# Value products of two neighbouring pairs issued together in the local attention units

## The reference

```python
# layer 1, x is 8 x 512 x 128
scores = einsum('bhtd,bhsd->bhts', q, k) * 8 ** -0.5
allowed = (j <= i) & (j >= i - 128)
attn = softmax(where(allowed, scores, -inf))
x = layernorm(x + einsum('bhts,bhsd->bhtd', attn, v) @ w_out)
# layer 2
h = layer_norm(x); x1 = x + causal_attention(h) @ w_o
xf = layer_norm(x1); top two of softmax(xf @ w_gate)
x = layernorm(x + x1 + sum over experts of gate * (gelu(xf @ w1 + b1) @ w2 + b2))
```

## Time and profile before

| | us |
|---|---|
| median of three runs | 866.76 |
| lowest and highest | 863.17, 868.02 |
| span of the profiled execution | 868.6 |
| TensorE matmul busy | 655.7 (75%) |
| VectorE busy | 509.7 (59%) |
| ScalarE busy | 462.6 (53%) |
| GpSimd busy | 429.8 (49%) |
| mean granted TensorE clock | 0.897 |

### The profile page before, as it was taken

How to read it: one execution, slowest core, us unless ns; L and a number is a source line. 1 busy time by engine, 2 the same in 40 slices (tenths; PEclk the granted TensorE clock), 3 DMA queues, 4 the chain that set the end, 5 groups by cost and what they waited for, 6 DMA issues and landing times.

```text
span 868.6 us, 19900 instructions
## 1 busy us (share of the span) xinstructions
PE 655.7 (75%) x7512; PEld 393.1 (45%) x7512; DVE 509.7 (59%) x1116; ACT 462.6 (53%) x671; POOL 429.8 (49%) x649
## 2 busy tenths in 40 slices
PE   2557978978887878888788888886614999999900
PEld 0323434434443433444343444442313998898900
DVE  1644667676776888798888879882340222222236
ACT  2035655655674565766677666666502554554503
POOL 4015556556654543245464647458640454445445
PEclk8568999998997998999999999999855999999965
DMA  5635544643643637334362707101014566566464
GB/s 170 157 90 115 138 109 100 154 126 67 159 116 46 153 97 135 102 76 135 66 159 42 185 25 190 43 16 53 20 58 161 187 204 214 184 223 213 168 163 128
DMA packets 73583, 107.45 MB, mean 124 GB/s; under 512 B 8104, under 2 KB 60048, under 8 KB 70428
## 3 DMA queue, kind: packets, MB, share of 16 engines
q1 hardware_dynamic: 68892, 97.86, 42.2%
q0 software_dynamic: 4608, 8.47, 3.3%
HBM read 44.14 MB, written 38.90 MB: 96 GB/s over the span
## 4 chain that ended last, share of the span: by engine, by line
PE 32%; DMA 22%; DVE 17%; issue 10%; SPq 7%; POOL 6%; ACT 4%; another core or an unknown queue 0%; POOLq 0%; ACTq 0%; DVEq 0%
DMA parts_dram<-parts 9%; DMA arena<-parts_dram 7%; PE pair_ps L1415 6%; PE o_ps L1278 6%; SPq L439 4%; PE o_ps L1434 3%; PE pair_ps L1299 3%; PE pair_ps L1198 3%; POOL rows_dram L628 3%; DMA rows_dram<-rows,row_at 3%; PE misc L1434 3%; DVE row_max L878 2%; ACT probs L707 2%; DVE row_max L876 2%; PE pair_ps L1258 1%
## 5 line engine op out<-in xcount | busy, mean ns | idle before, releaser
L707 ACT ACTIVATE probs<-pair_ps 128x1024 f32<-128x1024 f32 x272 | 275.4, 1022 | 116.2 <-PE pair_ps L1198 107.5
L1278 PE MATMUL o_ps<-probs,v_aug 128*32 128x256 f32 (+3 forms) x2048 | 166.0, 421 | 9.1 <-POOL probs L616 3.5
L603 POOL TENSOR_SCALAR_AFFINE_SELECT probs<-probs 128x512 f32<-128x512 f32 x96 | 61.2, 637 | 140.4 <-ACT probs L707 139.4
L1198 PE MATMUL pair_ps<-arena 50*128 50x256 bf16 (+3 forms) x1024 | 108.2, 288 | 26.6 <-DMA arena<-shift_t 6.5
L673 POOL DMA_INDIRECT outputs_dram<-o_norm,arena x80 | 77.7, 971 | 100.5 <-DVE o_norm L1128 80.0
L867 DVE TENSOR_REDUCE row_max<-pair_ps 128x4 f32<-128x768 f32 x96 | 89.7, 953 | 46.7 <-PE pair_ps L1232 46.1
L838 ACT ACTIVATE probs<-pair_ps,arena 128x256 f32<-128x256 f32 x160 | 65.4, 471 | 76.3 <-PE pair_ps L1415 66.0
L876 DVE TENSOR_REDUCE row_max<-pair_ps 128x2 f32<-128x1024 f32 x64 | 77.2, 1219 | 15.8 <-PE pair_ps L1258 14.7
L1415 PE MATMUL pair_ps<-x_t,arena 128*128 128x256 f32 x320 | 80.8, 397 | 7.1 <-DMA arena<-pack 3.9
L1198 PEld LDWEIGHTS pair_ps<-arena 50*128 50x128 bf16 x1024 | 32.7, 95 | 108.9 <-issue 45.5
L1278 PEld LDWEIGHTS o_ps<-probs,v_aug 128*32 128x32 f32 x2048 | 48.6, 111 | 66.0 <-issue 39.5
(11 more groups left out here) (147 smaller groups left out, 1107.8 us busy)
## 6 DMA issues: line engine op xcount, KB each, us to landing
arena<-pack SPq DMA_DIRECT2D x40, 578.0 KB
arena<-parts_dram SPq DMA_DIRECT2D x96, 192.0 KB
parts_dram<-parts SPq DMA_DIRECT2D x32, 384.0 KB
parts_dram<-parts SPq DMA_DIRECT2D x32, 256.0 KB
arena<-rows_dram SPq DMA_DIRECT2D x40, 130.0 KB
pack<-in_pack SPq DMA_DIRECT2D x8, 578.0 KB, 7.4
parts_dram<-parts SPq DMA_DIRECT2D x32, 128.0 KB
arena<-parts_dram SPq DMA_DIRECT2D x32, 128.0 KB
```

Source lines behind the costliest of these rows:

```text
L707: nc.scalar.activation(probs[:, n % PROBS, :], pair_ps[RING_AT["score", n][0]][:, :, :].rearrange("p b t -> p (b t)"), ACT.Exp, scale=SCAL ...
L1198: last = nc.tensor.matmul(pair[:, r, col:col + width], k_st[u % STACKS][own, gs, j * P:(j + 1) * P], q_st[u % STACKS][own, gs, q0:q0 + wid ...
L1278: last = nc.tensor.matmul(o_ps[c * VHEAD:(c + 1) * VHEAD, q0:q0 + width], v_aug[u % 2][:, j, first:first + VHEAD], probs[:, slot, r * T + ...
```

## The change

For a local unit `values_of` returned fourteen lists of one pair. Now it returns four lists in a half: pair 0 alone, then 1 and 2, 3 and 4, 5 and 6 (7; 8 and 9; 10 and 11; 12 and 13 in the second half). The semaphore `pv_done` counts lists, and the counts that depend on it (`VALUES_BEFORE`, `HALF_VALUES`, `VALUE_OF_PAIR`) follow from the table. Causal units and the experts are the same.

```diff
 def values_of(kind):
 
     if kind == LOCAL:
-        return [(k,) for k in range(14)]
+        return [tuple(7 * half + k for k in ks) for half in range(2) for ks in ((0,), (1, 2), (3, 4), (5, 6))]
     return [tuple(5 * g + k for k in ks) for g in range(4) for ks in ((0, 1), (2, 3), (4,))]
```

## The result

The changed kernel takes 876.1 us (median of 4 runs, 872.12 to 877.79) where the kernel before takes 864.96 (4 runs, 861.83 to 868.02): 1.2% slower, ratio 1.0121, 95% interval 1.0081 to 1.0162. The forecast was 869.7, with a range up to 875. The direction was right, the size was not: the difference of the medians is 11.1 us, against 2.9 worked out.

A forecast was written before the change was run, and what follows sets the result against it. The prediction took the kernel as bound by a loop of transfers (projection to landing) and engines (landing to projection); delays in the latter summed to +2.9 us on the 866.76 median, giving 869.7, range 864 to 875.

The forecast's parts named there:

- Bound and stretches: Eight local iterations loop through projection to landing, set by transfers, and landing to next projection, 6.8 us, set by engines.
- Gain of joining: Two value products in a row save 0.14 us of TensorE time, 4.5 us in all; only 2.2 around the landing could count.
- Step 11, the dear part: Pair 8, issued behind the landing, delays everything queued after it on TensorE by 0.43 us at full clock, 0.86 at half.
- the sum: Delays over local iterations 0 to 7: 0 + 0.86 + 0.43 + 0.43 + 0.2 + 0.8 - 0.2 + 0.4 = +2.9 us.
- B: Stretch from the landing of the stacks to the next projection, set by engines: 6.8 us at full clock, 7.9 at half.
- Steps without a product: Steps 12 and 0 lose their product (0.57 us in step 12), a gain only where TensorE is last, otherwise longer waits.
- Stretch A and its cover: Before the landing, late matmuls cost nothing in six of eight iterations, under waits of 1.59 us or more growing by 0.43.
- A: Stretch from a projection to the landing of the stacks, set by transfers: 23.3 us in the unit read.
- Clock: Behind landings, idle of that length may go either way; a drop to half costs 1.1 us, 1.5 with a double product.
- R1: Rival, 25%: the clock falls more often, at full-clock landings in iterations 2, 3 and 5; 872 to 876 us.
- R2: Rival, 12%: TensorE sets the stretch from landing to projection, so joining makes the kernel faster; 861 to 865.5 us.
- R3: Rival, 18%: nothing is left, the 0.43 us disappears in varying transfers or clock luck; 865.5 to 868 us.

The follow-up runs named there:

- filled changed kernel: The changed kernel with extra matmuls ahead of the landing, 20 in the first local iteration, 15 in the seventh, otherwise 13: 858.8 us, 1.0049 of the kernel before.
- sized fills: Extra matmuls ahead of the landing, 20 in the first iteration, 15 in the seventh, otherwise 9 (kernel before, 855.82 us) or 13 (changed kernel, 858.8 us).

## Why the prediction was wrong

*Bound and stretches: right.* The loop of transfers from projection to landing and of engines from landing to projection holds, and joining the second half of a unit alone costs 9.4 us.

*Gain of joining: right and worth nothing.* In the filled changed kernel the double product takes 1.00 us in the chain of waits, as in the earlier trace rows, and a wait of 0.53 follows in the step that has none.

*Step 11, the dear part: right, in mechanism and in size.* 7.21 against 6.78 us at the full clock is the 0.43 of the forecast; with sized fills on both sides the whole change costs 3.0 us, interval 1.0 to 5.0, for the 2.9 of the sum. That the sum comes out is in part luck. In the two filled profiles B grows by 0.43 in iterations 1 to 4 and by 0.81 in 5, but by 0.86 in 7, and it shrinks by 0.12 in 0 and by 0.54 in 6; the sum had 0.86 in 1, 0.2 in 4, 0.4 in 7 and -0.2 in 6, and these misses cancel.

*Steps without a product: right.* They give nothing back; the projection waits 1.14 us for VectorE where 1.1 was forecast.

*Stretch A and its cover: this is where it failed.* I wrote that late matmuls there cost nothing "under a wait of 1.59 us or more that grows by 0.43". The wait grew by 1.2 to 1.6 us in iterations 1 to 4. Part is arithmetic that I had in hand and didn't apply: pair 8 leaves 0.43, and the joined pairs 3 and 4 and 5 and 6 bring TensorE earlier to step 11 by 0.14 each, 0.71 in all. (Pairs 1 and 2 give nothing, since pair 1 stood with pair 0 before. Pair 12, which comes into A behind the projection, costs nothing there: the maxima of step 2 wait for an exponential and start 6.81 us behind the projection in both profiles.) From the start of the projection to the last scores' end it takes 21.3 us before and 20.4 after in iteration 2. The rest is in the transfers: A itself is 0.6 to 0.9 us longer in iterations 1 to 3, 0.4 of it in iteration 3 from the projection at half clock. Whether the change makes them longer, or this profile happened to have slow ones, is open; between kernels with the same stores and loads A differs as much.

*Clock: the term of the sum that was left at nothing, and the larger failure.* The likeliest case counted no more drops than before; R1 had the mechanism and named the three ends, with a quarter of the chance, and 872 to 876. Its price held: B of 8.68 at half against 7.21 at full is 1.5 us, as forecast, and a projection that falls to half costs 1.8 more. What was undersized is how often. Three ends (iterations 2, 3, 5) that were at full clock lost it in whole or part, and the projection of iteration 4 with them. Without extra matmuls the change costs 11 us; with seven and nine of them it costs 5.6, with sized ones 3.0. So 5.5 to 8 us, half to three quarters, came through the clock, with some 4 us to either side by the intervals. The profile of the changed kernel gives 5.9: B grew by 6.8, 4.1 more than the queue's 2.7, and the projection of iteration 4 by 1.8. Some 2.5 us of A's growth are left, and their cause is open. That the clock is a cause at all is shown by adding work to idle time.

The weighing was wrong: that 2.08 "was already enough once" and 2.45 "was once not enough" says that the waits before stood at the edge, so that one longer by any amount, as nearly all are after, should have counted as the likeliest case and not as a rival. The profiles of the seven kernels without extra matmuls (56 ends) say the same: of 8 waits under 1.5 us 7 were followed by a B at full clock throughout, of 17 between 1.5 and 2.5 us 5, of 31 over 2.5 us one. What decides within the middle group is open; the kernel with only pair 8 moved lost the clock behind 1.82 and 2.09 us, where the kernel before kept it behind 1.59, 2.21 and 2.45. R1's own sum, 874.1, is 2 us below the measured time.

The rule of the Trainium skill that I quoted against the change ("TensorE: Matmul & The Clock Gate", section "HAM oscillation — how this bites in real kernels") points the right way: waits for transfers between bursts of matmuls bring the half clock, and here that is the larger part of the loss. The waits in the page's own case are of about 3 to 5 us; here ends lost the clock behind waits of 1.75 to 2.5 us too, and others kept it.

*R2 and R3* are out: nowhere is B shorter by the joining, except by 0.3 us in the end of iteration 0, at half clock both times, where TensorE is last as R2 has it (and in iteration 6, where the clock differs too). In the chances, nine tenths of R1 and a fifth of the forecast make 31.5%, not 33; nothing here hangs on it.

## What to carry to other kernels

Ahead of a wait for a transfer, idle time is free and every product that can stand there should; behind the wait, put only what the next chain needs, and move the products behind the start of that chain (that gave 0.4% here without any fill, where the joining cost 1.2%). Idle time on TensorE isn't free in its length: work taken out of it can cost the clock for what follows, several times the time of the work moved (1.5 us for an end here, for 0.43 moved). Before a change makes such a wait longer, read the granted clock behind each wait that there is; where some lose it and others don't, price the drop as the likely case.

## What the hardware showed unexpectedly

Adding work made the kernel faster: 56 matmuls whose results nobody reads (7 in each of 8 iterations, 1.7 us together each time at the full clock) took 3.6 us off the kernel before, 0.9927 to 0.9985 of its time. And the clock reaches into the transfers' stretch: where a projection fell to half clock (up to 3.8 us instead of 1.95), the A that it starts took 24.7 to 26.9 us, otherwise mostly 23 to 24. Whether an end at half clock makes such a projection more likely is not shown: over all fourteen profiles it stands behind 7 of 60 ends at full clock and 7 of 52 others.
